# A transformer block on one core: the last chunk's output projection in two halves, its experts with relu and sigmoid on ScalarE and plain fp32 second products

## What is computed

```python
x = x + attn(layernorm(x))                   # out @ Wo.T + bo ends it
xc = layernorm(x).astype(bf16)
nf = (xc * rsqrt(mean(xc * xc) + EPS) * norm_weight).astype(bf16)
logits = nf @ gate_weight.T + gate_bias      # 8 experts
combine = softmax of the two largest logits, zero for the others
for e in range(8):
    p1 = nf @ mlp1_weight[e].T + mlp1_bias[e]
    g = minimum(p1[..., 0::2], 7)
    lin = clip(p1[..., 1::2], -7, 7)
    act = g * sigmoid(1.702 * g) * (lin + 1)
    combined += combine[e] * (act @ mlp2_weight[e].T)
x = x + (xc + combined.astype(bf16))
```

## Time and profile before

| | |
|---|---|
| time, median of 3 runs | 1096.22 us (1094.28 to 1101.87) |
| time of the profiled execution | 1097.99 us |
| its span, first to last instruction | 1096.2 us |
| busy: PE, DVE, ACT, POOL | 85%, 71%, 68%, 39% |
| mean granted TensorE clock | 0.945 of full speed |
| attention ends, chunk 7's projection starts | near 983 us, 999.4 us |
| chunk 7's experts start, end | near 1022 us, 1090 us |

### The profile page before, as it was taken

How to read it: one execution, slowest core, us unless ns; L and a number is a source line. 1 busy time by engine, 2 the same in 40 slices (tenths; PEclk the granted TensorE clock), 3 DMA queues, 4 the chain that set the end, 5 groups by cost and what they waited for, 6 DMA issues and landing times.

```text
span 1096.2 us, 16606 instructions
## 1 busy us (share of the span) xinstructions
PE 936.0 (85%) x5217; PEld 397.8 (36%) x5288; DVE 773.4 (71%) x1528; ACT 747.1 (68%) x1017; POOL 425.3 (39%) x357
## 2 busy tenths in 40 slices
...
GB/s 165 100 150 92 97 132 83 121 72 112 109 92 107 122 123 70 106 100 107 115 87 139 104 114 55 112 108 103 128 98 95 107 138 93 86 93 39 48 59 19
DMA packets 79984, 109.76 MB, mean 100 GB/s; under 512 B 22530, under 2 KB 56722, under 8 KB 76818
## 3 DMA queue, kind: packets, MB, share of 16 engines
...
## 4 chain that ended last, share of the span: by engine, by line
PE 58%; DVE 16%; issue 9%; ACT 6%; POOL 4%; DMA 3%; SPq 1%; ACTq 0%; another core or an unknown queue 0%; POOLq 0%; DVEq 0%
PE OP L726 16%; PE S L712 15%; PE D L698 9%; PE BB L681 4%; PE A L681 4%; PE D L600 3%; ACT probs L853 3%; PE D L622 3%; DVE th_sb L1159 3%; DVE acc L1154 2%; DVE l_sb L1144 2%; DVE g_sb L1142 2%; PE D L614 2%; DMA o_scr<-O 1%; ACT sqs L816 1%
## 5 line engine op out<-in xcount | busy, mean ns | idle before, releaser
L853 ACT ACTIVATE probs<-S 128x1024 f32<-128x1024 f32 x512 | 513.2, 1024 | 155.9 <-PE S L712 155.1
L712 PE MATMUL S<-Qs,Ks 98*128 98x512 bf16 x1024 | 301.6, 387 | 23.8 <-ACT probs L853 19.8
L726 PE MATMUL OP<-probs,V 128*17 128x512 f32 x2048 | 276.3, 612 | 3.6 <-ACT O L862 3.6
L940 POOL TENSOR_TENSOR act_lo<-act_sb,act_hi 128x512 fp32r<-128x512 f32 x128 | 171.6, 1343 | 150.6 <-ACT act_hi L842 143.9
L698 PE MATMUL D<-W,act_hi 128*128 128x256 f32 x448 | 133.4, 329 | 25.4 <-issue 14.4
L1154 DVE SCALAR_TENSOR_TENSOR acc<-D,combh,acc 128x256 f32<-128x256 f32 x224 | 97.6, 477 | 81.3 <-PE D L698 80.9
L712 PEld LDWEIGHTS S<-Qs,Ks 98*128 98x128 bf16 x1024 | 79.0, 99 | 203.9 <-ACT probs L853 98.7
L1159 DVE SCALAR_TENSOR_TENSOR th_sb<-th_sb,g_sb 128x512 f32<-128x512 f32 x128 | 122.7, 959 | 16.2 <-ACT th_sb L829 12.5
L934 POOL TENSOR_SCALAR W<-W2b 128x512 fp32r<-128x512 bf16 x64 | 43.1, 673 | 198.7 <-PE D L698 193.3
L698 PE MATMUL D<-W,act_lo 128*128 128x256 f32 x448 | 114.8, 287 | 0.0
L842 ACT CAST act_hi<-act_sb 128x512 fp32r<-128x512 f32 x128 | 78.4, 612 | 50.9 <-DVE act_sb L1164 45.4
...
## 6 DMA issues: line engine op xcount, KB each, us to landing
...
```

The costliest lines, as they stand in the source:

```text
L712: last = mm(S[:, j2, C * i:C * (i + 1)], Ks[0:SROWS + MROWS, g % 2, j, P * kt:P * (kt + 1)], Qs[0:SROWS + MROWS, g % 2, j, :], start=True, ...
L726: last = mm(OP[32 * j:32 * j + VW, :], V[:, kt, HG * g + j, :], probs[:, s % 2, C * j:C * (j + 1)], start=kt == 0, stop=kt == KT - 1)
L853: nc.scalar.activation(probs[:, s % 2, 2 * C * j2:2 * C * (j2 + 1)], S[:, j2, :], ACT.Exp, scale=SCALE).then_inc(exp_done, 1)
L940: tt(act_lo[:, e % 2, it, :], act_sb[:, a % 2, :], act_hi[:, e % 2, it, :].bitcast(FP32), ALU.subtract).then_inc(lo_s, 1)
```

## The change

Four things, all in the tail:

1. **Projection.** A new piece `wo_0` in half step 8 multiplies the half c = 0 of `Op` for both parts into the score banks `S`, ahead of chunk 6's last four downs; `wo` then adds c = 1 alone. Each part has its own pair of banks, so the second no longer waits until the first is read.
2. **Activation.** For the last chunk, ScalarE evicts the gate product with relu (7 - g is relu of 7 - p1 - b) and takes sigmoid of it; VectorE's `g_sb` step goes. VectorE makes (g_sb - 7) * sigmoid, and `combh` holds -1 times the weight.
3. **Downs.** The hidden tile is written once in fp32 (into `sw` and `rot`, which are free by then) and multiplied as plain fp32: four matmuls for eight, and `act_hi` and `act_lo` go.
4. **Order.** `final` of chunk 6 on VectorE stands behind `nf` of chunk 7.

Two small constants (`b1r`, `top_arg`) are made once on VectorE, early in the kernel.

```diff
-          "guard": 4, "flag": 6, "x1_in": 0, "x1_b": 11, "wo0": 13, "wo1": 14, "stats2": 15, "rstd2": 16, "xc": 17, "ss":
+          "guard": 4, "flag": 6, "x1_in": 0, "wo_0": 8, "x1_b": 11, "wo0": 13, "wo1": 14, "stats2": 15, "rstd2": 16, "xc": 17, "ss":
...
+        def wo_bank(u, a, bank):
+            if alone(u):
+                return S[:, a, :].rearrange("p (t c) -> p t c", t=2)[:, :, 0:E]
+            return bank[:, :].rearrange("p (t c) -> p t c", t=2)
+        def hidden_of(u, f):
+            e, it = divmod(f, 2)
+            return (sw, rot)[e % 2][:, it, :] if alone(u) else act_sb[:, it, :]
...
+                elif st == "wo_0" and alone(u):
+                    pe.wait_ge(exp_done, PAIRS * B * NCH)
+                    pe.wait_ge(on_s, 2 * u + 1)
+                    project_out(0, u, (0,), None)
+                    project_out(1, u, (0,), None)
                 elif st == "wo":
                     pe.wait_ge(on_s, 2 * (u + 1))
...
+                    project_out(a, u, (1,) if alone(u) else range(CT), bank).then_inc(d_full, 1)
...
                 if hh == 0:
-                    pe.wait_ge(lo_s, NF * u + m + 2)
+                    pe.wait_ge(act_s if alone(u) else lo_s, NF * u + m + 2)
...
+                    if alone(u):
+                        for it in range(2):
+                            last = mm(bank[:, E * q:E * (q + 1)], hidden_of(u, 2 * e + it)[:, tok:tok + P],
+                                      W2[:, e % 2, E * it:E * (it + 1)].bitcast(FP32), start=it == 0, stop=it == 1)
+                        continue
...
+                elif st == "up" and alone(u):
+                    e, it = divmod(a, 2)
+                    act.wait_ge(m1_mm, 2 * (NF * u + a) + 1)
+                    act.wait_ge(act_s, NF * u + a - 1)
+                    nc.scalar.activation(g_sb[:, a % 2, :], expert_banks(u, a)[0], ACT.Relu, bias=b1r[:, e, it:it + 1],
+                                         scale=-1.0).then_inc(g_s, 1)
+                    act.wait_ge(g_s, NF * u + a + 1)
+                    nc.scalar.activation(th_sb[:, a % 2, :], g_sb[:, a % 2, :], ACT.Sigmoid, bias=top_arg[:, 0:1],
+                                         scale=-ALPHA).then_inc(th_s, 1)
...
-                elif st == "lo":
+                elif st == "lo" and not alone(u):
...
+                    if alone(u):
+                        final(u - 1, n - 1)
                 elif st == "logits":
...
-                elif st == "final":
+                elif st == "final" and (looped(u) or u != B * NCH - 2):
...
-                v.tensor_scalar(combh[:, :, :], oh1[:, :, :], 0.5, None, ALU.mult).then_inc(comb_s, 1)
+                v.tensor_scalar(combh[:, :, :], oh1[:, :, :], -1.0 if alone(u) else 0.5, None, ALU.mult).then_inc(comb_s, 1)
...
+                    if alone(u):
+                        v.scalar_tensor_tensor(th_sb[:, q, :], g_sb[:, q, :], LIMIT, th_sb[:, q, :], ALU.subtract, ALU.mult).then_inc(t1_s, 1)
...
+                    if alone(u):
+                        dve.wait_ge(m2_mm, NF * u + 2 * (e - 1))
```

More of the change, by code:

```diff
@@ L74, in block_kernel @@
         place(PREP, h + AT["length"] + AT[st], (st, 0))
-    for st in ("x1_in", "x1_b", "stats2", "rstd2", "xc", "ss", "ms", "rrms", "nf", "nfT", "logits", "gates1", "etop",
+    for st in ("x1_in", "wo_0", "x1_b", "stats2", "rstd2", "xc", "ss", "ms", "rrms", "nf", "nfT", "logits", "gates1", "etop",
                "gates2", "combT"):
@@ L584, in stage @@
                 u = NCH * bb + n
-                if st in FILLS and filling[1] and (st != "guard" or n == NCH - 1):
+                if st in FILLS and filling[1] and (st != "guard" or n == NCH - 1) and not (st == "wo" and alone(u)):
                     pe.wait_ge(*read_of(*filling[1]))
@@ L658, in stage, with project_out @@
                     expert_down(a, u)
+            def project_out(a, u, parts_in, bank):
+                for t in range(2):
+                    tok = P * (2 * a + t)
+                    for c in parts_in:
+                        last = mm(wo_bank(u, a, bank)[:, t, :], Op[:, c, tok:tok + P], wo_sb[:, c, :],
+                                  start=c == 0, stop=c == CT - 1)
+                return last
             def expert_up(f, u):
@@ L822, in stage @@
                     nc.scalar.activation(etop[:, :], dtop[:, :], ACT.Exp).then_inc(etop_s, 1)
-                elif st == ("hidden" if alone(u) else "hi"):
+                elif st == "hi" and not alone(u):
                     upper_half(a, u)
-                elif st == "tanh":
-                    act.wait_ge(g_s, NF * u + a + 1)
-                    if looped(u) or u or a >= 2:
-                        act.wait_ge(act_s, NF * u + a - 1)
-                    nc.scalar.activation(th_sb[:, a % 2, :], g_sb[:, a % 2, :], ACT.Tanh, scale=ALPHA / 2).then_inc(th_s, 1)
+                elif st == "up" and alone(u):
[7 more added lines that the diff above has]
+                                         scale=-ALPHA).then_inc(th_s, 1)
+                elif st == "tanh":
+                    if not alone(u):
+                        act.wait_ge(g_s, NF * u + a + 1)
+                        if looped(u) or u or a >= 2:
+                            act.wait_ge(act_s, NF * u + a - 1)
+                        nc.scalar.activation(th_sb[:, a % 2, :], g_sb[:, a % 2, :], ACT.Tanh, scale=ALPHA / 2).then_inc(th_s, 1)
                     e, it = divmod(a, 2)
@@ L1043, in stage @@
                     dve.wait_ge(d_full, k + 1)
-                    xh = X1s[:, n, 2 * a:2 * a + 2, :].rearrange("p t c -> p (t c)")
-                    v.tensor_tensor(xh, bank[:, :], xh, ALU.add).then_inc(x1_s, 1)
+                    xh = X1s[:, n, 2 * a:2 * a + 2, :]
+                    v.tensor_tensor(xh, wo_bank(u, a, bank), xh, ALU.add).then_inc(x1_s, 1)
                 elif st == "stats2":
@@ L1137, in expert @@
                 if st == "up":
-                    dve.wait_ge(m1_mm, 2 * n + 1)
                     if looped(u) or u or f >= 2:
                         dve.wait_ge(act_s, n - 1)
-                    v.tensor_scalar(g_sb[:, q, :], gate, b1f[:, e, 0, it:it + 1], LIMIT, ALU.add, ALU.min).then_inc(g_s, 1)
+                    if not alone(u):
+                        dve.wait_ge(m1_mm, 2 * n + 1)
+                        v.tensor_scalar(g_sb[:, q, :], gate, b1f[:, e, 0, it:it + 1], LIMIT, ALU.add, ALU.min).then_inc(g_s, 1)
                     dve.wait_ge(m1_mm, 2 * n + 2)
```

19 lines of the change are left out of this document (9 added, 10 removed).

## The result

The changed kernel took 1080.14 us (median of 4 runs, 1079.13 to 1083.63), the kernel before 1096.16 (4 runs). The ratio is 0.9846, 95% interval 0.9818 to 0.9874: 16 us faster, where 1080.0 was forecast. Its profiled execution took 1079.36 us with a span of 1077.6, against 1097.99 and 1096.2.

What follows compares the result with a forecast made beforehand. The prediction took VectorE to bound chunk 7's experts and TensorE the projection, with a chain of waits at the end. Savings of 4.4 + 1.15 + 0 + 8.5 + 2.1 = 16.15 us gave 1080 us, range 1075.5 to 1088.

Steps and rivals of the forecast that it cites:

- 1. Projection: Chunk 7's projection: half the matmuls made early, GpSimd's bias add late next; saving 4.4 us, between 4.0 and 4.6.
- A faster clock on TensorE would add nothing: Chunk 7's projection: no further saving from TensorE's clock, since GpSimd binds.
- 2. `final` behind `nf`: VectorE between statistics and logits: nf starts 1.5 us earlier, logits wait 0.35 us; saving 1.15 us, 0.8 to 1.5.
- 3. Start of the experts: Up to down 0: table load and slower down against g_sb steps saved; 0, from 1 us gained to 1.8 lost.
- the second rival: Start of the experts: the table switch has a hidden second part, 1.4 us more bare, 1081.4; chance 0.13.
- 4. The tiles: Chunk 7's experts: 2.85 us a tile without g_sb on VectorE; saving 8.5 us, bounds 9.7 and 5.5.
- the first rival: Chunk 7's tiles: VectorE and TensorE, both full, take turns, 3.2 to 3.4 us a tile, 1084 to 1086.7; chance 0.12.
- The half clock: Rival, chunk 7's tiles: TensorE stays at half clock, 5.5 us a tile; 26 us slower with all sixteen; chance 0.05.
- 5. The end: Eviction of down 12 to down 15: 6.0 us for 8.1; saving 2.1 us, 2.4 at best, 0 to -1.5 at half clock.
- The sum: Whole tail: 4.4 + 1.15 + 0 + 8.5 + 2.1 = 16.15 us saved, median 1080.
- The bad end of the sum: Whole tail, all bad ends together: 4.0 + 0.8 - 1.8 + 5.5 + 0 = 8.5 us saved (1087.7).
- The fourth rival: Projection not on the path as read: projection and final's move give 1 us for 5.5, 1084.6; chance 0.05.

Runs made afterwards that it cites:

- e4: Changed kernel with the last chunk's downs again eight fp32r matmuls of act_hi and act_lo, relu and sigmoid kept: 1090.59 us, ratio to before 0.9944.
- e1: Changed kernel with chunk 7's whole projection put back behind the last Op: 1086.69 us (one run).
- e2: Changed kernel with final of chunk 6 put back ahead of nf of chunk 7 on VectorE: 1079.99 us (one run).
- e7: Changed kernel plus an unused GpSimd step of act_lo's shape per tile but the last, timed to meet th_sb: 1090.00 us (one run).
- e8: Changed kernel plus an unused GpSimd step of act_lo's shape per tile but the last, timed to meet l_sb and the eviction: 1079.93 us (one run).
- e5: Changed kernel with GpSimd's bias add for chunk 7 moved two half steps forward: 1083.72 us (one run).
- e6: Changed kernel with one product of every chunk 7 down made twice, two more TensorE records: 1084.32 us (one run).
- e3: Changed kernel with tanh and VectorE's g_sb step put back, plain fp32 downs kept: 1090.23 us, ratio to before 0.9942.

## Why the prediction held, point by point

**1. Projection: 4.4 forecast, 4.44 measured**, and by the path it named: the bias add of GpSimd is late next. That the digits agree is in part luck, with the clock before and with the scatter below. "A faster clock on TensorE would add nothing" is shown by e4, where the late halves took 3.68 us at the half clock and the stretch was 6.29 us, against 1.99 and 6.28 in the changed kernel. How much of it belongs to the change depends on the clock that the kernel before gets (3.2 us against e1). What the step lacked is the scatter of 0.86 us by which of two engines is held.

**2. `final` behind `nf`: 1.15 forecast, 1.31 measured**, 1.5 by e2. The mechanism was right, two sizes in it were not. rrms took 1.01 us, not 1.43, and `nf` 2.37, not the 1.6 assumed: rrms is longer beside `final` (1.38 us again in e2; by what wasn't tested), and in the changed kernel `nf` meets two W2 conversions. In e4, e7 and e8, where it meets one, it takes 2.02 us, and from `nf` to the logits it is 4.76 us for 5.12. That `lgb` would come right behind `final` is as forecast; so the 0.7 us on `nf` are paid in full.

**3. Start of the experts: 0 forecast, 0.87 gained.** All but 0.52 us of the table load was covered, at the first `th_sb`. Down 0 took 1.89 us at the full clock; I had allowed for the half. The stretch goes with that clock: it is 15.25 and 15.29 us in the two traces of the changed kernel, where down 0 took 1.89 us, and 16.14 to 16.24 in e1, e2 and e5, where the experts are the same and down 0 took 2.44 to 2.53; before it was 16.12. So the 0.87 is luck with the clock as much as it is the change, and it lies in the range of -1.8 to 1 that was given. The drain behind the load, the second rival, isn't there: the relu ahead of the load ends at 1019.00, and the sigmoid starts at 1020.31, where the load's 1.28 us from 1019.02 end. The 1.38 us of the Trainium skill ("ScalarE: Activation LUTs", "What ACT_TABLE_LOAD costs") are in no row here.

**4. The tiles: 8.5 forecast, 8.52 measured.** 2.85 us a tile was the estimate, 34.15 / 12 = 2.85 the mean. Its parts are different, and that they add up to the same is partly luck: VectorE's four steps are 2.77 us without a stall, not 2.90, and two tiles are held by 0.45. TensorE needs 2.60, not 2.75, so there was 0.17 us of play; taking turns, the first rival, is answered by e6. The half clock didn't come (1.00 from 1030 to 1064 us). What the step didn't say, and what I got wrong again in e4, is that its saving of 0.66 us has a condition. I took the removal of `act_lo` as a small extra on GpSimd and the fp32 downs as a cost to TensorE that is paid back at the end. In fact with the split downs the shorter tile on VectorE is filled up by the wait for GpSimd's ports: 3.43 us a tile in e4.

**5. The end: 2.1 forecast, 2.12 measured.** 6.00 us as worked out, last hidden step, two downs at the full clock, a tail. It needs both halves too: e3, with fp32 downs but VectorE longer, takes 7.59 us, with 2.76 us of idle TensorE and a half clock at first behind it.

**The sum** by the stretches is 17.3 us for 16.15 forecast, and the medians differ by 16.0. The part beyond the sum is nearly all the start of the experts and lies within the scatter of single traces. The bad end of the sum, 8.5 us, took 0 for point 5, whose own low bound is -1.5; with that it is 7.0 us. The fourth rival (the projection isn't on the path) fell with points 1 and 2.
